# A fused Mamba and feed-forward kernel: other places for the chunk's jobs, and another place for the copy of a state's last column

## The reference

```python
xz = einsum('btd,pd->btp', x, W_xproj)          # 64 rank columns, then B and C, 16 each
dt = softplus(einsum('btr,dr->btd', xz[..., :64], W_dt) + b_dt)
dA = exp(dt[..., None] * -exp(A_log))
dBx = dt[..., None] * B[:, :, None, :] * x[..., None]
h = dA_t * h + dBx_t                             # for each t, in order
y = einsum('bds,bs->bd', h, C_t)
x1 = layernorm(x + y + Dp * x)
hid = silu(x1 @ wg.T) * (x1 @ wu.T)              # weights / 127
out = layernorm(x1 + hid @ wd.T)
```

## Time and profile before

| | us |
|---|---|
| median of 3 runs | 1930.44 (1929.3 to 1931.55) |
| the profiled execution | 1934.14 |
| its span, first to last instruction | 1932.4 |
| VectorE busy | 1715.8 |
| TensorE busy | 1692.2 |
| GpSimd busy | 1641.3 |
| ScalarE busy | 1586.5 |

### The profile page before, as it was taken

One profiled execution on the slowest core, in us unless ns is written; L12 is line 12 of the kernel. 1 busy time (PEld: TensorE's weight loads), 2 busy tenths in 40 slices (PEclk: granted clock), 3 DMA queues, 4 the chain that ended last, 5 costly groups with the idle time before them and its releaser, 6 DMA issues. The chain is left out here.

```text
span 1932.4 us, 33150 instructions
## 1 busy us (share of the span) xinstructions
PE 1692.2 (88%) x11048; PEld 1347.9 (70%) x11048; DVE 1715.8 (89%) x2060; ACT 1586.5 (82%) x2992; POOL 1641.3 (85%) x710
## 2 busy tenths in 40 slices
PE   6788989988989888989888989888989888989877
PEld 4676777776777766777666777766777666777755
DVE  4888999999899898999999899998999999899993
ACT  6779888888888889888888888888888888888863
POOL 5988898988898988988988898988988988898960
PEclk7999999999999999999999999999999999999989
DMA  7322443223443223444233444223444233433200
GB/s 250 96 98 84 138 136 129 92 88 108 138 133 133 88 85 115 138 133 132 87 91 111 138 133 131 86 86 119 138 133 131 83 91 116 138 133 121 67 12 22
DMA packets 107419, 216.51 MB, mean 112 GB/s; under 512 B 10129, under 2 KB 44530, under 8 KB 107250
## 3 DMA queue, kind: packets, MB, share of 16 engines
q1 hardware_dynamic: 107250, 214.39, 34.6%
HBM read 195.48 MB, written 18.87 MB: 111 GB/s over the span
## 5 line engine op out<-in xcount | busy, mean ns | idle before, releaser
L408 POOL TENSOR_TENSOR h<-h,c_bc 128x1024 f32<-128x1024 f32 x352 | 830.3, 2368 | 114.4 <-DVE h L699 60.5
L398 POOL TENSOR_TENSOR ub<-u,b_bc 128x1024 f32<-128x1024 f32 x320 | 753.9, 2370 | 0.1
L922 PE MATMUL p_y<-ident,h 128*128 128x128 f32 x4096 | 522.7, 277 | 30.9 <-POOL h L408 29.5
L504 ACT ACTIVATE p_da<-dt,neg_a 128x512 f32<-128x512 f32 x640 | 435.2, 683 | 137.1 <-DVE h L699 133.4
L922 PEld LDWEIGHTS p_y<-ident,h 128*128 128x128 f32 x4096 | 473.6, 143 | 77.5 <-POOL h L408 38.3
L699 DVE TENSOR_TENSOR_SCAN h<-p_da,h_carry,ub 128x512 f32<-128x512 f32 x320 | 394.9, 1269 | 19.0 <-ACT p_da L504 19.0
L699 DVE TENSOR_TENSOR_SCAN h<-p_da,ub 128x512 f32<-128x512 f32 x320 | 376.2, 1209 | 26.6 <-ACT p_da L504 21.7
L518 ACT ACTIVATE ub_t<-u_t,bc_t 128x256 f32<-128x256 f32 x768 | 345.8, 499 | 0.0
L977 PE MATMUL p_o<-wt_down,hid 128*128 128x256 f32 x1536 | 342.5, 379 | 2.4 <-DVE res L740 1.6
L977 PEld LDWEIGHTS p_o<-wt_down,hid 128*128 128x128 f32 x1536 | 289.0, 190 | 54.6 <-issue 14.7
L504 ACT ACTIVATE da_k<-dt,neg_a 128x512 f32<-128x512 f32 x384 | 267.8, 714 | 0.0
(11 more groups left out here) (91 smaller groups left out, 1643.0 us busy)
## 6 DMA issues: line engine op xcount, KB each, us to landing
c_bc<-bc_rows_dram SPq DMA_DIRECT2D x352, 256.0 KB, 6.4
b_bc<-bc_rows_dram SPq DMA_DIRECT2D x64, 768.0 KB, 6.6
b_bc<-bc_rows_dram SPq DMA_DIRECT2D x64, 512.0 KB, 4.0
x_in<-in_L_attn_x SPq DMA_DIRECT2D x32, 512.0 KB, 6.2
out_x<-res_n SPq DMA_DIRECT2D x32, 512.0 KB, 3.3
bc_rows_dram<-bc_rows SPq DMA_DIRECT2D x32, 64.0 KB, 1.7
hid<-in_L_ffn_w_gate SPq DMA_DIRECT2D x1, 768.0 KB, 5.1
hid<-in_L_ffn_w_up SPq DMA_DIRECT2D x1, 768.0 KB, 6.9
```

The costliest lines, as they stand in the source:

```text
L398: nc.gpsimd.tensor_tensor(ub[:, i % UB_SLOTS, :, :], u[:, par, :, :], b_bc[:, i:i + 1, :].broadcast_to([P, DH, T]), ALU.mult).then_inc(s_u ...
L408: nc.gpsimd.tensor_tensor(h[:, s % H_SLOTS, :, :], h[:, s % H_SLOTS, :, :], c_bc[:, i:i + 1, :].broadcast_to([P, DH, T]), ALU.mult).then_i ...
L504: nc.scalar.activation(da, dt[:, par, q, :], ACT.Exp, scale=neg_a[:, q, s:s + 1]).then_inc(done, 1)
L922: ins = nc.tensor.matmul(p_y_tok[:, k, q * P:(q + 1) * P], h[:, s % H_SLOTS, q, k * P:(k + 1) * P], ident[:, :], start=(s == SUM_ORDER[0] ...
```

## The change

Jobs of `AT` stand at other places; state 9's decays are made three units ahead instead of one, state 15's one instead of two. `carry` was the last instruction of zone 3 of its own unit and is now issued in zone 0 of the next unit, behind the jobs and the products of that zone. Slots are counted through all chunks, and chunk numbers in addresses are plain integers. Left out below is the replacement of a slot's formula by `k_slot` and `ub_slot` in five more places and of `isinstance(c, int)` in the waits.

In the order of the queues, before and after, around unit 10: ScalarE before `silu0 | silu1 silu2 silu3 | norm2_0 | silu4 carry 9 || (10) | silu5 exp_table decay 11.0 | | decay 11.1 carry 10`, after `carry 8 | silu0 silu1 | bc_cols silu2 | || (10) silu3 silu4 silu5 exp_table carry 9 | decay 11.0 | | decay 11.1`. TensorE before `gate0 gate1 | transposes 10.0 | gate2 gate3 || (10) transposes 10.1 | gate4 gate5 up0`, after `gate0 gate1 transposes 10.0 || (10) transposes 10.1 | gate2 | gate3 gate4 gate5 up0 up1`. VectorE before has hidden0 behind scan 10.1 and hidden1 in unit 12, after both stand ahead of scan 11.0.

```diff
--- before.py
+++ after.py
@@ -23,6 +23,8 @@
+CARRY_LAG = 1
+CARRY_ZONE = 0
...
@@ -30,20 +32,20 @@
-    "weights": (7, 1), "x_transposed": (1, 3), "x_out": (1, 3), "project": (2, 1), "rank_out": (3, 2),
-    "bc_out": (3, 1), "project_dt": (3, 2), "softplus_abs": (4, 3), "softplus_exp": (5, 1),
-    "softplus_log": (6, 1), "dt_of": (6, 2), "u_of": (5, 1), "u_transposed0": (11, 4), "u_out0": (14, 0),
-    "u_transposed1": (14, 3), "u_out1": (15, 1), "z_out": (2, 3), "stats1": (3, 1), "mean1": (5, 2),
-    "norm_log": (5, 2), "norm_exp": (5, 3), "shifts": (6, 1), "norm1_0": (6, 1), "norm1_1": (6, 2),
-    "norm1_2": (6, 3), "norm1_3": (7, 1), "x1_transposed": (7, 1), "x1_high": (7, 3), "x1_low": (9, 0),
-    "gate0": (9, 2), "gate1": (9, 2), "gate2": (9, 4), "gate3": (9, 4), "gate4": (10, 1), "gate5": (10, 1),
-    "silu0": (9, 0), "silu1": (9, 1), "silu2": (9, 1), "silu3": (9, 1), "silu4": (9, 3), "silu5": (10, 1),
-    "exp_table": (10, 1), "up0": (10, 1), "up1": (11, 0), "up2": (11, 1), "up3": (13, 2), "up4": (13, 4),
-    "up5": (14, 1), "hidden0": (10, 2), "hidden1": (12, 2), "hidden2": (13, 1), "hidden3": (13, 2),
-    "hidden4": (15, 0), "hidden5": (15, 0), "skip0": (7, 1), "skip1": (6, 2), "down0": (1, 0), "down1": (1, 1),
-    "down2": (1, 1), "down3": (1, 2), "down4": (3, 1), "down5": (3, 1), "down6": (3, 1), "down7": (3, 2),
-    "residual0": (1, 1), "residual1": (4, 1), "stats2": (5, 0), "mean2": (5, 2), "norm2_0": (9, 2),
-    "norm2_1": (11, 2), "norm2_2": (14, 1), "norm2_3": (15, 3), "bc_turned": (6, 1), "bc_cols": (11, 1),
+    "weights": (7, 1), "x_transposed": (0, 4), "x_out": (0, 2), "project": (2, 1), "rank_out": (4, 0),
+    "bc_out": (3, 1), "project_dt": (3, 3), "softplus_abs": (5, 1), "softplus_exp": (5, 1),
+    "softplus_log": (5, 3), "dt_of": (7, 0), "u_of": (7, 0), "u_transposed0": (12, 2), "u_out0": (14, 0),
+    "u_transposed1": (14, 3), "u_out1": (14, 2), "z_out": (2, 0), "stats1": (4, 0), "mean1": (5, 1),
+    "norm_log": (6, 0), "norm_exp": (6, 0), "shifts": (6, 1), "norm1_0": (6, 2), "norm1_1": (7, 1),
+    "norm1_2": (7, 1), "norm1_3": (7, 1), "x1_transposed": (8, 0), "x1_high": (8, 0), "x1_low": (8, 2),
+    "gate0": (9, 3), "gate1": (9, 3), "gate2": (10, 1), "gate3": (10, 2), "gate4": (10, 2), "gate5": (10, 2),
+    "silu0": (9, 1), "silu1": (9, 1), "silu2": (9, 2), "silu3": (10, 0), "silu4": (10, 0), "silu5": (10, 0),
+    "exp_table": (10, 0), "up0": (10, 2), "up1": (10, 2), "up2": (13, 0), "up3": (13, 1), "up4": (13, 4),
+    "up5": (14, 3), "hidden0": (11, 0), "hidden1": (11, 0), "hidden2": (13, 1), "hidden3": (14, 0),
+    "hidden4": (15, 0), "hidden5": (15, 0), "skip0": (8, 2), "skip1": (6, 1), "down0": (0, 3), "down1": (1, 0),
+    "down2": (1, 0), "down3": (1, 2), "down4": (2, 4), "down5": (2, 4), "down6": (3, 0), "down7": (3, 2),
+    "residual0": (1, 2), "residual1": (4, 2), "stats2": (5, 1), "mean2": (5, 2), "norm2_0": (11, 1),
+    "norm2_1": (11, 2), "norm2_2": (14, 3), "norm2_3": (15, 1), "bc_turned": (6, 0), "bc_cols": (9, 2),
...
@@ -52,7 +54,7 @@
-DA_LEAD = {6: 2, 10: 2, 14: 2, 15: 2}
+DA_LEAD = {6: 2, 9: 3, 10: 2, 14: 2}
...
@@ -257,6 +259,18 @@
+
+        def ub_slot(c, i):
+            return (NB * c + i) % UB_SLOTS
+
+        def k_slot(c, i):
+            return (NK * c + i) % K_SLOTS
+
+        def slot_freed(eng, states, c, i, slots):
+
+            n = len(states) * c + i - slots
+            if n >= 0:
+                eng.wait_ge(s_scan, DH * units(n // len(states), states[n % len(states)]))
...
@@ -314,13 +328,13 @@
-                sp.dma_start(out_chunks[bass.ds(c, 1)].rearrange("a p k d -> (a p) k d"),
+                sp.dma_start(out_chunks[c],
-                             x_chunks[bass.ds(c, 1)].rearrange("a p k d -> (a p) k d")).then_inc(s_x_in, 16)
+                             x_chunks[c]).then_inc(s_x_in, 16)
...
@@ -391,11 +405,8 @@
-                if i >= UB_SLOTS:
-                    wait(pool, s_scan, 2 * units(c, B_STATES[i - UB_SLOTS]))
-                else:
-                    wait(pool, s_scan, 2 * units(c - 1, B_STATES[i - UB_SLOTS + NB]))
-                nc.gpsimd.tensor_tensor(ub[:, i % UB_SLOTS, :, :], u[:, par, :, :],
+                slot_freed(pool, B_STATES, c, i, UB_SLOTS)
+                nc.gpsimd.tensor_tensor(ub[:, ub_slot(c, i), :, :], u[:, par, :, :],
...
@@ -493,11 +504,8 @@
-                    if i >= K_SLOTS:
-                        wait(act, s_scan, 2 * units(c, K_STATES[i - K_SLOTS]))
-                    else:
-                        wait(act, s_scan, 2 * units(c - 1, K_STATES[i - K_SLOTS + NK]))
-                    da, done = da_k[:, i % K_SLOTS, q, :], s_da_k[q]
+                    slot_freed(act, K_STATES, c, i, K_SLOTS)
+                    da, done = da_k[:, k_slot(c, i), q, :], s_da_k[q]
...
@@ -628,8 +636,10 @@
                                 ce, se, pe_ = unit_at(c, s, ahead, par)
                                 if DA_LEAD.get(se, 1) == ahead and core and (se >= ahead or nxt):
                                     decay(ce, se, pe_, zone // 2)
-                        if core and par == 0 and zone == 3:
-                            carry(c, s)
+                        if zone == CARRY_ZONE:
+                            cq, sq, pq = unit_at(c, s, -CARRY_LAG, par)
+                            if pq == 0 and (core if s >= CARRY_LAG else prev):
+                                carry(cq, sq)
 
             def tail(c):
                 z_out(c)
```

More of the change, by code:

```diff
@@ L81, in mamba_ffn_block @@
     NR = len(B_RUNS)
-    assert NB % UB_SLOTS == N % H_SLOTS == NK % K_SLOTS == 0
+    assert N % H_SLOTS == 0
     assert all(sum(AT[f"skip{a}"]) > max(SUM_LAG.values()) for a in range(2))
@@ L242, in wait @@
         def wait(eng, s, value):
-            if not isinstance(value, int) or value > 0:
+            if value > 0:
                 eng.wait_ge(s, value)
@@ L332, in broadcast_b @@
                 i, n = B_STATES.index(first), last + 1 - first
-                if not (isinstance(c, int) and c == 0):
+                if c > 0:
                     wait(sp, s_ub, NB * (c - 1) + i + n)
@@ L359, in step @@
                     broadcasts(c, par, LATE, 2 * N)
-                if nxt and not (isinstance(c, int) and c + 2 >= CHUNKS):
+                if nxt and c + 2 < CHUNKS:
                     load(c + 2)
@@ L517, in times_b @@
                 for k in range(2 * half, 2 * half + 2):
-                    nc.scalar.activation(ub_t[:, i % K_SLOTS, k, :], u_t[:, k, :], ACT.Identity,
+                    nc.scalar.activation(ub_t[:, k_slot(c, i), k, :], u_t[:, k, :], ACT.Identity,
                                          scale=bc_t[:, par, k, s:s + 1]).then_inc(s_ubt, 1)
@@ L681, in scan @@
                     wait(dve, s_ub_ps, DH * (k_units(c, s) - 1) + q + 1)
-                    da, dbx = da_k[:, K_STATES.index(s) % K_SLOTS, q, :], p_da[:, q, :]
+                    da, dbx = da_k[:, k_slot(c, K_STATES.index(s)), q, :], p_da[:, q, :]
                 else:
@@ L687, in scan @@
                         dve.wait_ge(s_ub, NB * c + (i + 1))
-                    da, dbx = p_da[:, q, :], ub[:, i % UB_SLOTS, q, :]
+                    da, dbx = p_da[:, q, :], ub[:, ub_slot(c, i), q, :]
                 if q == 0:
                     ch, sh, _ = unit_at(c, s, -H_SLOTS, par)
-                    if not (isinstance(ch, int) and ch < 0):
+                    if ch >= 0:
                         wait(dve, s_y, sums(ch, sh))
@@ L852, in x_transposed @@
                 pe.wait_ge(s_x_in, 16 * (c + 1))
-                if isinstance(c, int) and c < 2:
+                if c < 2:
                     wait(pe, s_dt, c)
-                elif isinstance(c, int) and c == 2:
+                elif c == 2:
                     pe.wait_ge(s_wt, 2 + WEIGHT_BATCHES)
@@ L896, in ub_transposed @@
                     ins = nc.tensor.transpose(p_da[:, q, k * P:(k + 1) * P],
-                                              ub_t[:, i % K_SLOTS, k, q * P:(q + 1) * P], ident[:, :])
+                                              ub_t[:, k_slot(c, i), k, q * P:(q + 1) * P], ident[:, :])
                 ins.then_inc(s_ub_ps, 1)
```

## The result

The changed kernel takes 1916.9 us (median of 7, 1909.7 to 1925.6) against 1930.4 us before: ratio 0.9924, 95% interval 0.9894 to 0.9953. The profiled execution took 1925.6 us, the slowest of the seven; that scatter, 16 us against 10 before, is part of the finding.

What follows compares the result with a forecast made beforehand. ScalarE's chain was taken to pace units 4 to 11. A pair gains 1.4 + 1.2 + 0.35 - 0.4 - 0.2 = about 2.4 us, 36 us over 30 chunks: 1895 us, own band 1875 to 1912, range 1862 to 1928.

Steps and rivals of the forecast that it cites:

- ScalarE's chain: Units 4 to 11: ScalarE's work sets the pace; reordering gains 1.4 us in even chunks and 1.2 in odd.
- VectorE waits for up0: Before hidden0, end of units 4 to 11: one wait of 2.5 to 3 us in place of three.
- The idle before the logarithm and before the residual: Units 4 to 11: ScalarE's wait for mean2 (0.98 even, 1.25 odd) and the residual's 0.96 us wait both go.
- Units 11 to 0: Stretch where VectorE was full: odd chunks gain 0.35 us, even chunks lose 0.4.
- the late decay of state 13: Units 11 to 0: with hidden1 gone, the scan waits 0.25 us (odd) or 0.5 (even) for the second decay.
- the copy ahead of state 12's product: Units 11 to 0, even chunks: last-column copy moves behind state 15's products, delaying VectorE's product; 0.45 us lost.
- GpSimd's wait for the copy of state 9: Unit 10, even chunks: copy comes about 1.7 us later relative to the silus; hidden, 1.5 us to spare.
- rival C: Units 0 to 4: z_out blocks ScalarE ahead of state 3's decay; 2 us delay gives 1954 us; chance 0.12.
- GpSimd has room: GpSimd's queue at u: state 4's product fills its 3.48 us idle, with no cost charged.
- the four rivals: TensorE replaces the silus (0.14); VectorE is the bound (0.08); z_out makes it slower (0.12); work only shuffled inside waits (0.08).
- rival A: At gate2: TensorE takes the silus' place, a chunk gains only 0.3 to 0.6 us, 1912 to 1926; chance 0.14.
- gate2 behind scan 9.1: Units 4 to 11, odd chunks: gate2 starts at 22.3 where 21.55 would be possible, 0.75 us lost.

Runs made afterwards that it cites:

- psum_operand: Changed kernel with the small VectorE instruction shift reading p_da (PSUM) instead of mean_var, so not computed from the mean; 1870.3 us, ratio 0.9710.
- one_operand: Changed kernel with shift reading only mean_var, the factor rstd left out, its waits, place and size unchanged; 1917.6 us, ratio 0.9931.

## Why the prediction was wrong

**Right.** That ScalarE's chain paces units 4 to 11: with the shift's wait gone the stretch is 28.2 us in both kinds of chunk, and VectorE waits for up0, 1.73 us in the odd and 2.09 in the even chunk shown (forecast 2.5 to 3), where three waits stood. The idle before the logarithm and before the residual is gone. Units 11 to 0 came out at 15.5 and 15.7 (forecast 15.55 and 15.7), with both losses where they were put: the late decay of state 13 (0.14 us odd, 0.22 even; forecast 0.25 and 0.5) and the copy ahead of state 12's product (0.40; forecast 0.45). GpSimd's wait for the copy of state 9 rose from 1.73 to 3.03 us, by 1.3 where 1.7 were forecast, and that copy starts 0.02 us behind the table load (989.07 behind 987.77 + 1.28). One sign of rival C is there without its cost: ScalarE waits 1.1 to 1.3 us at z_out in every chunk, and scan 3 waits for nothing.

**The step that failed.** "GpSimd has room: it idled 3.48 us at u, where state 4's product now runs first." I costed this move at nothing, since I looked at GpSimd alone. The idle that it filled stood beside an instruction of VectorE, shift, which took 0.14 us there and which my sum does not name. Now it takes 2.49 us, 2.35 more on the path of each odd chunk, and in some chunks the clock falls long in TensorE's longer wait and costs 1.1 more. psum_operand shows both at once: 46.6 us. None of the four rivals named it. The time lies in the band of rival A, by luck: A had a gate held by TensorE, and the failure lay ahead of the gates; A's upper end does not follow from its own gain either, since 1930 less 9 is 1921, not 1926. Two things on record before the change would have pointed at it: the 5.00 us of shift beside GpSimd's products in the last chunk, and its operands. Of the instructions that VectorE repeats, shift alone takes two tensors from SBUF; every other has one in PSUM or only one.

**A term too small.** Without that step the change brings 60 us (1930.4 to 1870.3), not 36. Per pair 116.1 became 112.5, 3.6 instead of 2.4 us. Units 4 to 11 gained 1.7 in each kind (forecast 1.4 and 1.2): of the 0.75 us that I charged in odd chunks for gate2 behind scan 9.1 some 0.2 appear (in psum_operand gate2 starts 0.93 us behind the first silu, at 898.14, where I had 0.74 as the least). Units 0 to 4 gained 0.3 in odd chunks where I had none. The two errors have opposite signs, so that the time fell inside the range for the wrong reason: without the first, 1870 lies below the 1875 of the forecast's own band.

**The copy** was put at 0.4 us per even chunk, 6 us; it is 9 without and 13 with the shift's wait.

## What to carry to other kernels

When a move fills an engine's idle time, look not only at who waits for that engine but at what the others run at that moment; a tiny instruction of VectorE that reads and writes SBUF alone can wait out a whole instruction of GpSimd (2.35 us here), and two in a row at worst. Compare the mean length of each kind of instruction between two profiles before the waits: a longer "busy" can be a wait that has no row. Look also at the longest single row of a kind, not only at the mean. And an order of jobs that is good by durations and semaphores alone should be tried with its smallest instructions moved by a unit or given an operand in PSUM.

## What the hardware showed beyond what I expected

A small instruction of VectorE (128x8) took 2.46 to 2.49 us beside a GpSimd product of 2.35 us, and in two chunks 5.11 and 4.97 us, two products in a row: GpSimd can keep what VectorE waits for over the border of two of its instructions. Which borders VectorE wins I could not tell: in the even chunk shown it asked 0.57 us ahead of one and got it (0.59 us); where it took 5.11 and 4.97 us it had asked 0.49 and 0.33 us ahead and lost two; in one_operand it twice lost from 0.54 us ahead (2.87 us), from where it mostly won. At 0.10 to 0.15 us ahead it lost the next product in all 14 steady odd chunks of the changed kernel and in 13 of one_operand's 14 (2.43 to 2.50 us), and won once (0.15). So the distance alone does not decide it.

Around a wait of 3.3 us TensorE's granted clock was 0.50 for 6.8 us in eight chunks, for 3.4 us in four and not at all in two of the same execution; around one of 1.94 us it was 0.50 for 3.4 us or not at all; waits of 0.96 and 1.04 us left it at 1.00 in the chunks shown. The eight long falls began inside the wait, some 1 us before its end, the four short ones between 0.6 us before and 1.4 us behind it. At half clock the sixteen products behind the wait took 3.62 instead of 1.91 us. What decides between a long, a short and no fall is not shown. The changed kernel scattered by 16 us in seven executions (1909.7 to 1925.6), and by 2 in four with the hole filled; the long falls account for some 9 us in the slowest execution, and the rest of the scatter stays open.
